# The pair stage of a mixture of experts: its side work at other pairs and in four banks

## The reference, cut to what matters

```
s1  = xn + o @ Wo                                  # o: gated output of the recurrent attention, normed by head
xn2 = s1 * rsqrt(mean(s1^2) + 1e-5) * ln2_w        # the second norm
s   = s1 + (silu(xn2 @ W1) * (xn2 @ W3)) @ W2      # MLP, hidden width 704
routed = sum over 4 of 64 experts: share * (silu(xn @ wg[e]) * (xn @ wu[e])) @ wd[e]     # hidden width 64
shared = sum over 2 shared experts: (silu(xn @ swg) * (xn @ swu)) @ swd                  # hidden width 256 each
x   = x + s * silu(routed + shared)
```

## Time and profile before

| | |
|---|---|
| median of three runs | 1204.97 us |
| the three runs | 1199.20, 1204.97, 1209.54 us |
| the profiled execution, its own time | 1213.53 us |
| its span in the profile | 1211.8 us |
| mean granted clock of TensorE | 0.933 |
| PE busy | 1061.9 us (88%) |
| DVE busy | 853.6 us (70%) |
| ACT busy | 627.6 us (52%) |
| POOL busy | 563.2 us (46%) |
| the pair stage in it | 990.3 to 1147.4 us |

### The profile page before, as it was taken

The page is one execution under the profiler, slowest core; times in us unless marked ns, Lnnn a source line. Parts: engine busy times, 40 slices in busy tenths (PEclk is TensorE's granted clock), DMA queues, the critical chain, the costliest instruction groups (busy, mean ns, idle before and its releaser), DMA issues. The chain is left out here.

```text
span 1211.8 us, 23405 instructions
## 1 busy us (share of the span) xinstructions
PE 1061.9 (88%) x7870; PEld 703.4 (58%) x7870; DVE 853.6 (70%) x1509; ACT 627.6 (52%) x1241; POOL 563.2 (46%) x401
## 2 busy tenths in 40 slices
PE   6876978999999999699999999989969677797797
PEld 4455766666666666466666666559525254465444
DVE  4967327778887788488778787845689846675566
ACT  3536147666666666466666666633521035454441
POOL 3630335667665776377558664524075002220063
PEclk9875789999999999899999999999979878899898
DMA  5135021786877655536685656651113056567632
GB/s 166 52 109 154 27 53 14 96 85 98 70 89 98 77 94 63 99 66 71 88 101 76 82 64 85 88 114 39 53 75 115 20 185 200 160 188 247 218 94 81
DMA packets 186058, 119.82 MB, mean 99 GB/s; under 512 B 64548, under 2 KB 179286, under 8 KB 185686
## 3 DMA queue, kind: packets, MB, share of 16 engines
q1 hardware_dynamic: 170070, 97.35, 45.3%
q10 hardware_dynamic: 12800, 12.58, 3.0%
q0 software_dynamic: 3072, 8.39, 2.0%
HBM read 81.90 MB, written 36.37 MB: 98 GB/s over the span
## 5 line engine op out<-in xcount | busy, mean ns | idle before, releaser
L1297 DVE TENSOR_REDUCE a_nmax<-psum 128x1 f32<-128x1024 f32 x128 | 156.1, 1220 | 78.1 <-PE psum L1145 77.9
L1303 DVE SCALAR_TENSOR_TENSOR a_pT<-psum,a_pT 128x512 f16<-128x512 f32 x256 | 164.8, 684 | 22.0 <-ACT a_pT L1240 13.9
L1240 ACT ACTIVATE a_pT<-psum 128x512 f16<-128x512 f32 x256 | 140.2, 604 | 15.0 <-PE psum L1156 11.1
L1232 ACT ACTIVATE a_ex<-psum,a_nmax 128x1024 f32<-128x1024 f32 x128 | 142.8, 1116 | 9.8 <-issue 9.3
L1058 POOL TENSOR_TENSOR a_rnorm<-a_ss,a_power 128x8 f32<-128x8 f32 x32 | 58.4, 1825 | 177.8 <-DVE a_ss L1273 177.8
L1156 PEld LDWEIGHTS psum<-ident,a_ex 128*128 128x128 f32 x1024 | 119.5, 141 | 25.4 <-DVE a_pT L1303 0.7
L1156 PE MATMUL psum<-ident,a_ex 128*128 128x128 f32 x1024 | 133.1, 273 | 0.0
L1127 PE MATMUL psum<-a_wh,xT_h 128*128 128x128 f16 (+1 forms) x512 | 115.5, 248 | 2.0 <-PEq L2724 2.0
L1128 PE MATMUL psum<-a_wl,xT_h 128*128 128x128 f16 (+1 forms) x512 | 115.4, 248 | 0.0
L1129 PE MATMUL psum<-a_wh,xT_l 128*128 128x128 f16 (+1 forms) x512 | 115.4, 248 | 0.0
L1167 PE MATMUL psum<-a_pT,a_vh 128*128 128x512 f16 x256 | 98.1, 383 | 14.2 <-DVE a_of L976 13.2
(11 more groups left out here) (394 smaller groups left out, 2588.5 us busy)
## 6 DMA issues: line engine op xcount, KB each, us to landing
split_gate_up<-a_e_wh SPq DMA_DIRECT2D x64, 128.0 KB
a_rb<-row_scales SPq DMA_DIRECT2D x32, 256.0 KB
g_e_gu<-split_gate_up SPq DMA_DIRECT2D x32, 256.0 KB, 3.6
block_outputs<-g_e_ym ACTq DMA_DIRECT2D x16, 512.0 KB, 4.5
split_rest<-a_e_wh SPq DMA_DIRECT2D x45, 128.0 KB
wf<-in_L_ffn_W_gate SPq DMA_DIRECT2D x32, 128.0 KB, 2.4
wf<-in_L_ffn_W_up SPq DMA_DIRECT2D x32, 128.0 KB, 2.5
wf<-in_L_ffn_W_down SPq DMA_DIRECT2D x32, 128.0 KB, 2.8
```

Source lines behind the costliest of these rows:

```text
L1232: act.activation(ex[m % 2][:, :], score_banks(m), ACT.Exp, bias=nmax[:, m % 2:m % 2 + 1], accum_out=total[g][:, k:k + 1]).then_inc(exp_rea ...
L1240: act.activation(pT[g][:, 0, 4 * h:4 * h + 4, (m % 4) * P:(m % 4 + 1) * P], bank_of(r, unit).rearrange("p (k q) -> p k q", k=4), ACT.Copy, ...
L1297: dve.tensor_reduce(nmax[:, k:k + 1], score_banks(m), AX.X, ALU.max, negate=True).then_inc(max_ready, 1)
L1303: dve.scalar_tensor_tensor(low, bank_of(r, unit).rearrange("p (k q) -> p k q", k=4), PROB, high, ALU.mult, ALU.subtract).then_inc(low_done, 1)
```

## The change

The constants become `GATE_EVERY, TURN_OUT, PRODUCT, DOWN, TURN2, AHEAD = 2, 13, 17, 40, 32, 3`. So the shared experts' gate/up products stand in pairs 0, 2, ... 14; their down products in pairs 40 to 47, the last copy to `mix` behind the loop; the residual adds and squares in pairs 20 to 27; the scaling of the mean squares in pair 28; the turns of the normed tiles in pairs 32 to 39, their high parts in 33 to 40, their low parts in 36 to 43 as before. The Wo products, the normed tiles' turns and the down products each go round banks 4 to 7 instead of two banks, so each waits for the reader of four before instead of two before, and the first four of each wait for the last readers of the work ahead of them in the same banks. The gated tiles' turns keep banks 6 and 7. GpSimd's eight halves are issued without the loop over pairs, in the same order.

```diff
     def down_slot(self, n):
-        return self.psum[:, 4 + n % 2, 0:D]
+        return self.psum[:, 4 + n % 4, 0:D]
 
     def down(self, pe, n):
         pe.wait_ge(self.hl_ready, 2 * self.QUARTERS)
-        if n == 0:
-            pe.wait_ge(self.up_done, 2 * self.QUARTERS)
-        if n >= 2:
-            pe.wait_ge(self.y_done, n - 1)
+        if n >= 4:
+            pe.wait_ge(self.y_done, n - 3)
...
-    GATE_EVERY, TURN_OUT, PRODUCT, DOWN, TURN2, AHEAD = 3, 13, 17, 26, 34, 2
+    GATE_EVERY, TURN_OUT, PRODUCT, DOWN, TURN2, AHEAD = 2, 13, 17, 40, 32, 3
...
+    def side_bank(n):
+        return psum[:, 4 + n % 4, 0:D]
...
                 dve.wait_ge(y_ready, n + 1)
-                dve.tensor_tensor(s1[:, n, :], spare(n), xn[:, n, :], ALU.add).then_inc(s_done, 1)
+                dve.tensor_tensor(s1[:, n, :], side_bank(n), xn[:, n, :], ALU.add).then_inc(s_done, 1)
...
             def side(q):
                 if PRODUCT + AHEAD <= q < PRODUCT + AHEAD + NT:
                     add_residual(q - PRODUCT - AHEAD)
-                if TURN2 + AHEAD <= q < TURN2 + AHEAD + NT:
-                    low(q - TURN2 - AHEAD)
+                if TURN2 + 1 + AHEAD <= q < TURN2 + 1 + AHEAD + NT:
+                    low(q - TURN2 - 1 - AHEAD)
...
             pool.memset(xTs[:, :, SLOTS1:], 0.0).then_inc(tail_done, 1)
-            for q in range(PAIRS):
-                k, after = (q - 5) // GATE_EVERY, (q - 5) % GATE_EVERY
-                if 0 <= k < SHARED_HALVES:
-                    if after == 0:
-                        shared.hidden(pool, k)
-                    elif after == 2:
-                        shared.low(pool, k)
+            for k in range(SHARED_HALVES):
+                shared.hidden(pool, k)
+                shared.low(pool, k)
...
             blocks.store(act, PAIRS - 1)
+            shared.down_done(act, NT - 1, mix)
...
             def product(n):
                 pe.wait_ge(evac, NT)
-                if n >= 2:
-                    pe.wait_ge(s_done, n - 1)
+                if n == 0:
+                    pe.wait_ge(shared.up_done, SHARED_HALVES)
+                if n >= 4:
+                    pe.wait_ge(s_done, n - 3)
                 for c in range(DC):
-                    last = pe.matmul(spare(n), ogT[:, c, tokens_of(n)], wo[:, c, :],
+                    last = pe.matmul(side_bank(n), ogT[:, c, tokens_of(n)], wo[:, c, :],
...
             def turn_normed(n):
                 pe.wait_ge(x2r_ready, n + 1)
-                if n >= 2:
-                    pe.wait_ge(x2_low, n - 1)
+                if n < 4:
+                    pe.wait_ge(s_done, n + 5)
+                else:
+                    pe.wait_ge(x2_low, n - 3)
...
                 if DOWN <= q < DOWN + NT:
+                    if q - DOWN < 4:
+                        pe.wait_ge(x2_low, q - DOWN + 5)
                     shared.down(pe, q - DOWN)
```

More of the change, by code:

```diff
@@ L2296, in low @@
                 for c in range(DC):
-                    last = dve.scalar_tensor_tensor(x2T_l[:, c, tokens_of(n)], spare(n)[:, c * P:(c + 1) * P],
+                    last = dve.scalar_tensor_tensor(x2T_l[:, c, tokens_of(n)], side_bank(n)[:, c * P:(c + 1) * P],
                                                     ln[:, 1, c:c + 1], x2T_h[:, c, tokens_of(n)], ALU.mult, ALU.subtract)
@@ L2407, in high @@
                 for c in range(DC):
-                    last = act.activation(x2T_h[:, c, tokens_of(n)], spare(n)[:, c * P:(c + 1) * P], ACT.Copy,
+                    last = act.activation(x2T_h[:, c, tokens_of(n)], side_bank(n)[:, c * P:(c + 1) * P], ACT.Copy,
                                           scale=ln[:, 1, c:c + 1])
@@ L2494, in turn_normed @@
                 pe.wait_ge(x2r_ready, n + 1)
-                if n >= 2:
-                    pe.wait_ge(x2_low, n - 1)
+                if n < 4:
+                    pe.wait_ge(s_done, n + 5)
+                else:
+                    pe.wait_ge(x2_low, n - 3)
                 for c in range(DC):
-                    last = pe.transpose(spare(n)[:, c * P:(c + 1) * P], x2r[:, n, c * P:(c + 1) * P], ident[:, :])
+                    last = pe.transpose(side_bank(n)[:, c * P:(c + 1) * P], x2r[:, n, c * P:(c + 1) * P], ident[:, :])
                 last.then_inc(t2_ready, 1)
```

## The result

The kernel after took 1197.78 us (median, 1190.66 to 1205.61) against 1206.44 us for the kernel before in the same sessions (1199.20 to 1211.38). The ratio is 0.9934, 95% interval 0.9916 to 0.9953: 0.7% faster, some 8 us, where 1208.3 had been forecast: the sign was wrong. 1197.8 lies outside the 1201 to 1215 that the forecast gave itself and inside the 1196 to 1218 that the rivals had widened it to. The gain is under the 1%, 12 us, that the prediction took for the least that can be told from no change, but twenty executions of each kernel put the interval clear of 1.

The account below looks back on a forecast made before the run. PE was taken to bound the pair stage, then PE with DVE, then PE beside SP's queue. Terms 5.9 - 3.0 - 2.0 + 4.0 - 1.6 = +3.3 us on the 1204.97 median gave 1208.3; range 1196 to 1218.

Parts of the forecast that it names:

- Pairs 0 to 20 ... Sum +5.9: First pairs: three more gate/ups, two lost later, new waits, register loads left in place; +5.9 us.
- the array stays at its upper clock: Rival, first 59.7 us: denser gate/ups keep the clock up, this stretch -8.3, total 1194 us; chance 0.13.
- The turns and the new wait on `up_done`: Pairs 0 to 20: changed cover of gated turns' waits on ACT, +0.7; gate/up waiting for ACT's copies, +1.0 us.
- Pairs 21 to 29: PE loses a gate/up and two down products, DVE limits the gain, new wait for squares +0.5; sum -3.0 us.
- Pairs 29 to 39: Some 7 us of down products leave PE, but SP's load queue holds the gain to -2.0 us.
- Pairs 40 to 47: Eight down products enter the last pairs, partly filling PE's idle or waiting time: +4.0 us, ends +2.5 and +7.
- The block behind: First eight matmuls behind the pair stage run at clock 1.00 instead of 0.50: -1.6 us.
- Four banks take the waits away: Rival: with four banks PE's waits on DVE and ACT, 4.6 us, go; 1200 us; chance 0.13.
- The down products stand bare at the end: Rival, pairs 40 to 47: products cost their whole 10.4 us, pairs 21 to 39 return nothing; +16, 1221 us; chance 0.14.

Follow-up runs that it names:

- downs_only: Kernel before with only the shared down products moved to pairs 40 to 47, last copy behind the loop: 1206.18 us, 1.0002.
- after_again: The changed kernel once more, unchanged, for a second profile: 1199.33 us, 0.9944 of the kernel before.
- gates_only: Kernel before with only the shared gate/ups moved to every second pair (0, 2, ... 14), two banks: 1197.63 us, 0.9941.
- gates_downs: Kernel before with gate/ups every second pair and down products in pairs 40 to 47, but two banks and the norm where it was: 1200.65 us, 0.9963.
- after_downs_early: The changed kernel with the shared down products in pairs 25 to 32 instead of 40 to 47: 1197.71 us, 0.9944 of the kernel before.
- filler_behind: Kernel before with 24 useless matmuls directly behind the register loads of pairs 3, 6, 9 and 12: 1210.09 us, 1.0027.
- filler: Kernel before with 24 useless matmuls right ahead of the register loads of pairs 3, 6, 9 and 12: 1201.08 us, 0.9966.
- loads_behind_after: The changed kernel with the register loads moved behind the side work of their pair: 1192.24 us, 0.9888 of the kernel before.
- spread_downs: loads_behind_before with the shared down products in pairs 27, 30, 33, 36, 39, 42, 45 and 46 instead of 26 to 33: 1188.49 us, 0.9876.
- loads_behind_before: Kernel before with the register loads moved from ahead of their pair's down product to behind its side work: 1192.45 us, 0.9888.
- loads_split: Kernel before with a group's two register loads taken apart, behind the side work of pairs 3i and 3i + 1: 1188.71 us, 0.9889.

## Why the prediction was wrong, step by step

**The step that failed is "Pairs 0 to 20 ... Sum +5.9".** To the output of pair 19 the kernels with gate/ups every third pair in front of a bare load took 79.6 us (before) and 77.9 (downs_only); the five with the new placement 69.8 (after), 73.0 (after_again), 73.6 (gates_only), 71.4 (gates_downs) and 73.8 (after_downs_early). The means are 78.7 and 72.3, so the stretch gave 6.4 us back. Two things in the step were wrong:
- It says that the change leaves each register load where it is. In the code it does. But what a load costs depends on what stands ahead of it, and this the change moves. I had read the 25.0 us of the earlier trace rows, of which 22.8 stand at the reads, as a fixed price. PE's idle time in the stretch went from 16.5 and 15.0 us to 11.6 to 12.8, a mean of 12.5: -3.3 us. The two covered groups of reads, pairs 3 and 9, would by themselves give 4.4. That filler_behind keeps the gaps and filler closes half of them shows the order to be the cause.
- It prices a gate/up at the mean of the earlier trace rows, 3.73 us. They cost 2.76 to 2.77 in after and, but for one or two a profile, in the other four. The one that stays slow in all four is that of pair 12, 3.8 to 5.3 us, right behind the one long gap that the new placement leaves; in after it took 2.76 even there. The time at 1.2 GHz in the stretch fell from 30.8 and 29.1 us to 10.0, 22.6, 20.6, 13.4 and 19.5, mean 17.2. Half of the difference, 6.4 us, is at most what the lower clock had cost. PE's busy time fell from 63.0 to 59.8 us, a mean of -3.1, with one gate/up (2.8 us) more in it, so that 5.9 of the 6.4 came back. 2.8 - 5.9 - 3.3 = -6.4. The gate/up of pair 12 in gates_only (PE, columns as in the earlier trace rows):

```profile
1026.75:1031.85 5.10, 5.10 (x17) 0.53 0.31 89
```

The forecast had named a clock over 0.9 in the first 60 us as what would make it wrong, and that is what after shows (0.97 in its first 60 us); in the other four kernels with the new placement these 60 us show 0.87 to 0.90, against 0.81 before.

This is the rival "the array stays at its upper clock" in its size (its -8.3 for this stretch, 1194 us, against the 1197.8 measured), but not in its reason: it held that the register loads stay, and I gave it 0.13 for that. The rows that should have moved the chance were there: among the loads in the earlier trace rows those of pairs 3, 6 and 12 left PE idle for 3.25, 2.13 and 2.56 us, and the expensive gate/ups (5.21 us in the earlier trace rows, 4.4 and 4.9) are those of pairs 3, 6 and 12, right behind. The clock was low where the gap was. How much of the clock's part is due to the gaps closed and how much to the denser work, filler_behind (0.91 with the gaps left) and filler (0.96) let me bound but not separate; the clock also differs by itself, from 0.85 to 0.93 between two profiles of the same kernel, after_again and after:

```profile
992.80:1065.80 73.00, 61.39 (x505) 37.59 (x506) 48.96 (x122) 39.04 (x79) 21.31 (x16) 0.85 0.58 180
```

**The turns and the new wait on `up_done`** (+0.7, +1.0). Waits of after, who for whom, us in all, times, longest:

```profile
PE psum L2479 <- ACT g_ogT L2399: 3.7, 2, 2.0
PE psum L1565 <- ACT g_s_up L1576: 1.2, 3, 0.4
PE psum L1709 <- ACT g_e_ym L1728: 0.7, 1, 0.7
```

```profile
SPq L2372 <- DVE g_share L1529: 6.3, 1, 6.3
```

The turns' two waits are 3.7 us against 3.5, +0.2; the wait on `up_done` is new and 1.2 us in three places, as forecast.

**Pairs 21 to 29** (-3.0): right, though not by the down products. From the output of pair 19 to that of 28 it went from 25.4 and 24.6 us to 22.0, 21.2, 21.9, 21.1 and 22.2, a mean of -3.3. DVE's busy time in the stretch fell by 2.76 us (23.17 to 20.41), where 2.5 had been taken for GpSimd's four operations. gates_only, which keeps its down products there, has 21.9 us of the same; the two that leave are worth 0.8 (before against downs_only, gates_only against gates_downs). The new wait for the squares costs nothing: the scaling of the mean squares starts right behind the operation ahead of it (timeline of DVE in after).

```profile
1076.41 0.69 DVE L1527 TENSOR_TENSOR g_equal<-g_equal,g_r_prob 128x512 f32<-128x512 f32 x1
1077.13 0.17 DVE L2341 TENSOR_SCALAR g_ms<-g_ms 128x8 f32<-128x8 f32 x1
```

**Pairs 29 to 39** (-2.0): the mechanism was right. SP's queue paces the stretch. In after it waits for the last share (L2372, above), brings the first MLP piece at 1079.21, and gate/up 41 follows (timelines of SP and of PE's weight loads):

```profile
1079.21 0.58 SPq L2375 DMA_DIRECT2D g_mlp<-split_rest  x1
```

```profile
1109.26 0.77 PEld L1696 LDWEIGHTS psum<-g_xTs,g_e_gu 128*128 128x128 f16 x12
```

That is 30.05 us from one to the other. In before gate/up 41 began at 1126.32, 30.76 us after its release. In all fourteen profiles, whatever was moved, it lies between 28.3 and 31.1 us. But the share itself came later behind the output of pair 28, by 0.3 to 1.5 us against before, in four of the five kernels with the new gate/ups. From that output to gate/up 41 the five took 31.0, 30.3, 31.3, 30.8 and 30.1 us against 31.0 and 30.9: -0.3, inside the ends of that term; the 7 us of down products taken out turned into waits for loads, as said.

**Pairs 40 to 47** (+4.0): right within the spread. Gate/up 41 to the first MLP matmul took 22.1, 26.6, 27.4, 26.0 and 24.4 us in the five kernels with late down products (after, after_again, gates_downs, downs_only, loads_behind_after; mean 25.3) and 18.7 to 22.6 in the nine others (mean 21.0): +4.3. The timeline of ACT's outputs in after confirms both rates, about 2.5 us for a pair with a gate/up and a down product, 1.8 to 1.9 for the last two:

```profile
1120.55 0.60 ACT L1728 ACTIVATE g_e_ym<-psum 128x512 f32<-128x512 f32 x1
1123.05 0.60 ACT L1728 ACTIVATE g_e_yx<-psum 128x512 f32<-128x512 f32 x1
...
1127.44 0.60 ACT L1728 ACTIVATE g_e_ym<-psum 128x512 f32<-128x512 f32 x1 [1.00 <-PE psum L1709]
1129.23 0.60 ACT L1728 ACTIVATE g_e_yx<-psum 128x512 f32<-128x512 f32 x1 [0.92 <-PE psum L1709]
```

**The block behind** (-1.6): right. Its first 3.4 us run at 1.00 in all five kernels with late down products, and mostly or wholly at 0.50 in seven of the nine others; gates_only and spread_downs begin at 1.00. The windows of downs_only and after_downs_early, columns as in the earlier trace rows:

```profile
1153.30:1156.70 3.40, 3.39 (x16) 1.57 (x17) 0.00 (x0) 0.60 (x1) 0.99 (x1) 1.00 0.07 22
```

```profile
1135.20:1138.60 3.40, 3.37 (x8) 1.17 (x9) 0.00 (x0) 0.00 (x0) 1.02 (x1) 0.50 0.25 88
```

Twice as many matmuls in the same 3.4 us. The 1.6 us are what this start is worth; from the first matmul of the MLP to the end of the span it is 57.5 to 59.7 us in the seven profiles that begin at 1.00 and 59.7 to 64.3 in the seven others, so more may hang on it, which no run isolates.

**The sum**, with the measured terms: -6.4 - 3.3 - 0.3 + 4.3 - 1.6 = -7.3 us, against the 8.0 us that the ratio makes of 1206.44. With this one term of the forecast at its measured value, -6.4 for +5.9, its sum would have been +3.3 - 12.3 = -9.0.

**The rivals.** "Four banks take the waits away": after and gates_downs differ by no more than their intervals, and gates_only has the whole gain with two. The Trainium skill, "Perfetto Trace Analysis", Matmul Optimizations, asks for all eight banks in use; for this kernel the runs can't tell what four in turn are worth from nothing (gates_downs above). "The down products stand bare at the end" fell: downs_only is 1.0002 (0.9972 to 1.0032), and its cost of +4.3 less 1.6 at the start of the MLP and 0.8 in pairs 19 to 28 leaves 1.9 us, which that interval holds. The Trainium skill, "TensorE: Matmul & The Clock Gate", HAM oscillation, would have had the last eight pairs begin slow. From gate/up 41 on the clock is 1.00 in after and 0.88 to 0.98 in the four others with late down products, so the trace agrees in part.

What stays open: why gates_only (0.9941), without the late products' cost, isn't ahead of after, and after_downs_early isn't either. The terms above give them 2.7 us (+4.3 - 1.6), or 4.3 to gates_only, whose MLP begins at 1.00; intervals of ±2 to 3 us each don't show this with certainty. Open too is why the clock fell in one profile and not in another behind a gap of the same length.

## What to carry to other kernels

A register read in an engine's instruction list had no fixed price here: it was free behind wide matmuls and cost the array up to its whole length behind narrow ones, or where the sequencer had just stood in a wait. So put such reads last in an iteration, behind the widest work, and when costing a move look at what it puts ahead of or takes from the reads that stay. When expensive instances of an operation stand right behind idle gaps, ask what will stand there after the move: an instance without the gap cost the price at the upper clock, not the mean. Work taken out of a stretch that a DMA queue paces is worth nothing there, while what it fills elsewhere is charged in full.

The best version found is loads_behind_before (one line moved, 1.1% faster than before) or either of the two variants on it, spread_downs and loads_split, which can't be told from it.

## What the runs showed of the hardware that I had not expected

- Two small register reads left TensorE idle for up to 3.25 us, and a single read took 0.33 to 2.42 us. The Trainium skill, "DMA: Bandwidth & Descriptors", Latency and other measured facts, gives a floor of about 600 ns for such a load; the rows don't agree, with reads of 327 and 328 ns and a median of 544 in after.
- TensorE's sequencer ran ahead of its array by the length of what was queued: 1.9 us at pair 3 of after behind wide matmuls, 0.1 us at pair 3 of before behind narrow ones. The Trainium skill, "TensorE: Matmul & The Clock Gate", Architectural detail, gives the engine a queue of 64; the trace agrees in so far as the 33 weight loads and matmuls that stood ahead of the read and had not begun when it did are fewer.
- 24 useless matmuls, 5.5 us at the 2.76 us that twelve take, made the kernel about 4 us faster ahead of the reads and did not make it faster behind them.
- The time at 1.2 GHz in pairs 0 to 19 was 10.0 us in one profile and 22.6 in another of the same kernel, so one profile can't size the clock's part.
